# Spreading v over the key index by on-chip transfers into four slots in place of matmuls, with the normalised keys kept in PSUM, in a fused attention and mixture-of-experts layer

## The reference

```python
q = _silu(x @ Wq.T).reshape(b, n, H, HD)          # H = 16 heads, HD = 8
k = _silu(x @ Wk.T).reshape(b, n, H, HD)
v = _silu(x @ Wv.T).reshape(b, n, H, HD)
f = jax.nn.log_sigmoid(x @ Wf.T)
k = k / jnp.maximum(jnp.linalg.norm(k, axis=-1, keepdims=True), EPS_NORM)
# per head and token, in order of the tokens:
S = jnp.exp(ft)[..., None, None] * S + kt[..., :, None] * vt[..., None, :]
o = jnp.einsum('bhk,bhkv->bhv', qt, S)
...
# then: o normalised, gated with sigmoid(x @ Wg1.T @ Wg2.T), times Wo, added to x;
# layer norm and modulation; two shared experts and the best 2 of 8 experts per token,
# each silu(x @ w1.T) * (x @ w3.T) @ w2.T, hidden size 256; added to x
```

## Time and profile before

| | |
|---|---|
| three runs | 440.51 median, 438.13 to 441.07 us |
| profiled execution | 441.05 us, span 439.2 (1.85 us outside it) |
| PE busy | 382.0 us (87%), weight loads 292.8 (67%) beside it |
| DVE / ACT / POOL busy | 326.2 (74%) / 202.5 (46%) / 291.3 (66%) |
| starts of normalise_k, blocks 0 to 7 | 20.83, 45.05, 72.53, 105.43, 133.90, 161.86, 189.99, 217.97 us |

### The profile page before, as it was taken

One profiled execution on the slowest core, in us unless ns is written; L12 is line 12 of the kernel. 1 busy time (PEld: TensorE's weight loads), 2 busy tenths in 40 slices (PEclk: granted clock), 3 DMA queues, 4 the chain that ended last, 5 costly groups with the idle time before them and its releaser, 6 DMA issues. The chain is left out here.

```text
span 439.2 us, 8647 instructions
## 1 busy us (share of the span) xinstructions
PE 382.0 (87%) x2304; PEld 292.8 (67%) x2304; DVE 326.2 (74%) x941; ACT 202.5 (46%) x505; POOL 291.3 (66%) x373
## 2 busy tenths in 40 slices
PE   7768796869999999999987789788998998999875
PEld 3453453556775966868656468675887887888475
DVE  5789999876998989989899763534665665666535
ACT  3453343544456455553523343314554554555630
POOL 1155555785888887888968578752876878588600
PEclk8999999877999999999999598899999999999999
DMA  8800021000000000100000011122333333232197
GB/s 246 306 1 0 1 74 48 24 1 2 12 32 7 26 24 14 32 7 26 24 14 30 8 37 44 55 61 67 91 92 86 87 91 85 76 91 69 58 346 208
DMA packets 27808, 28.57 MB, mean 65 GB/s; under 512 B 4458, under 2 KB 21746, under 8 KB 27618
## 3 DMA queue, kind: packets, MB, share of 16 engines
q1 hardware_dynamic: 23442, 19.14, 15.0%
q0 software_dynamic: 4320, 8.89, 6.2%
HBM read 17.03 MB, written 12.03 MB: 66 GB/s over the span
## 5 line engine op out<-in xcount | busy, mean ns | idle before, releaser
L1406 POOL DMA_INDIRECT y_dram<-S x71 | 70.9, 999 | 17.7 <-issue 15.9
L1233 POOL TENSOR_TENSOR qS<-S,qT 128x512 f32<-128x512 f32 x56 | 74.3, 1330 | 10.4 <-DVE S L1550 10.2
L1255 POOL DMA_INDIRECT h_dram<-h,target_i x56 | 55.8, 996 | 15.4 <-issue 15.4
L1793 DVE COPY qS<-ff 128x256 f32<-128x256 f32 x71 | 30.2, 425 | 41.6 <-PE ff L880 41.6
L1537 DVE TENSOR_TENSOR at<-at,khat 128x512 f32<-128x512 f32 x64 | 44.0, 691 | 3.7 <-PE at L587 2.9
L1182 ACT ACTIVATE S<-ff 128x256 f32<-128x256 f32 x71 | 27.3, 384 | 34.4 <-PE ff L873 34.4
L1550 DVE TENSOR_TENSOR_SCAN S<-decay,S,at 128x512 f32<-128x512 f32 x32 | 40.8, 1274 | 0.6
L1550 DVE TENSOR_TENSOR_SCAN S<-decay,at 128x512 f32<-128x512 f32 x32 | 38.7, 1213 | 0.6
L1047 ACT ACTIVATE work<-ff 128x512 f32<-128x512 f32 x32 | 19.0, 595 | 39.3 <-PE ff L510 38.5
L871 PE MATMUL ff<-w_hi,vT_lo 128*128 x71 | 34.2, 482 | 3.2 <-issue 3.2
L586 PE MATMUL at<-vT_hi,spread_v 128*128 128x512 f32 x64 | 30.4, 476 | 7.2 <-DVE S L1550 5.6
(11 more groups left out here) (276 smaller groups left out, 1004.8 us busy)
## 6 DMA issues: line engine op xcount, KB each, us to landing
S<-h_dram SPq DMA_DIRECT2D x71, 64.5 KB, 1.9
xall<-in_x SPq DMA_DIRECT2D x8, 256.0 KB, 5.5
work<-in_w13T SPq DMA_DIRECT2D x8, 256.0 KB, 2.8
w_hi<-y_dram SPq DMA_DIRECT2D x8, 256.0 KB, 5.5
w_lo<-y_dram SPq DMA_DIRECT2D x8, 256.0 KB, 6.0
out<-xall SPq DMA_DIRECT2D x8, 256.0 KB, 3.1
w_sb<-in_w2T SPq DMA_DIRECT2D x1, 1280.0 KB, 6.8
y_dram<-S POOLq DMA_INDIRECT x71, 2.3
```

The costliest lines, as they stand in the source:

```text
L1233: pool.tensor_tensor(qS[:, v, :], S[:, v, :], qT[:, b % 2, :], ALU.mult).then_inc(s_qS, 1)
L1255: pool.indirect_dma_start(out=h_dram[:, :], out_offset=bass.IndirectOffsetOnAxis(ap=target_i[:, b % 2, k, t:t + 1], axis=0), in_=token_row ...
L1406: pool.indirect_dma_start(out=y_dram[:, :], out_offset=bass.IndirectOffsetOnAxis(ap=rows[:, u, P:P + 1].bitcast(I32), axis=0), in_=y_sb[:, ...
L1793: dve.tensor_copy(t_GT[:, u % RING, :], ff[2 + u % 2][:, 0:HID]).then_inc(s_tGT, 1)
```

## The change

v is no longer spread by PE. vT keeps two blocks (by b % 2), and SP's queue issues one transfer for each block and v: 16 rows of vT, those of value v, each copied to the 8 rows of its head in slot n % 4 of a new SBUF buffer `vs`, n = 8 b + v. A transfer waits until ACT has made vT of the block (s_act) and until update n-4 has read the slot. The six weight loads stand between the transfers of blocks 1 and 2. The parts of vT and `spread_v` are gone, with `split_v` on ACT and POOL.

`update` multiplies slot and keys into at[v%2], and waits for the transfer and for the scan that read the bank before. The keys stay in PSUM: `normalise_k` writes `kbank`, which is the bank that held the gathers' result (obank), and waits for updates 6 and 7 of the block before; update 7 of a block moves from the head of the next period to ahead of `normalise_k`. The gathers go to another bank (`bbank`), which the second silu pair and h also use, and both halves of block i-1 run in period i, between projections. v is projected second (ORDER), and ACT makes it ahead of the decay. The last query has a buffer of its own (q7). In the first period and period 1 matmuls without use (`keep_busy`) are placed anew; later periods have none.

```diff
-        ORDER = (1, 3, 2, 4, 0)
+        ORDER = (1, 2, 3, 4, 0)
...
+            def spread(b, v):
+                n = HD * b + v
+                if v == 0:
+                    sp.wait_ge(s_act, 5 * b + 2)
+                if n >= SPREAD:
+                    old_b, old_v = divmod(n - SPREAD, HD)
+                    sp.wait_ge(s_upd[half(old_v)], scans(old_b, old_v))
+                sp.dma_start(vs[:, n % SPREAD, :], vT[v:P:HD, b % 2, :].unsqueeze(1).broadcast_to([H, HD, TB])) \
+                    .then_inc(s_vs[n % SPREAD], 16)
...
+            for b in range(NB):
+                for v in range(HD):
+                    spread(b, v)
+                    if b == 1 and v >= HD // 2:
+                        load_w13(NSH + v - HD // 2 + 2)
+                    if b == 2 and v % 4 == 3:
+                        load_w13(NSH + v // 4 + 6)
...
             def gather(b, k):
                 if k == 0:
-                    wait(pe, s_og, b)
                     wait(pe, s_qS, (HD - 1) * b + HD // 2)
...
+                    if b < NB - 1:
+                        wait(pe, s_hrow, b - 1)
+                    else:
+                        pe.wait_ge(s_h2T, NB - 1)
...
             def period(i):
-                if i != 2:
-                    on(spread, i, 0)
                 on(up, i - 3, 2)
...
                 on(project, i + 1, 0)
-                on(spread, i, 1)
-                on(spread, i, 2)
+                on(gather, i - 1, 0)
                 on(project, i + 1, 1)
                 on(gather, i - 1, 1)
...
                 on(project, i + 1, 3)
                 on(logits, i - 2)
                 if i == 1:
-                    keep_busy(obank, 5)
-                on(spread, i, 6)
-                if i == 1:
-                    keep_busy(obank, 2)
-                on(spread, i, 7)
+                    keep_busy(ff[1], 7)
                 on(up, i - 2, 0)
...
                 on(transpose_x1, i + 2)
-                on(gather, i, 0)
...
             def update(b, v):
                 if v == 0:
                     wait(dve, s_khat, b + 1)
-                wait(dve, s_vb, HD * b + v + 1)
-                dve.tensor_tensor(at[half(v)][:, :], at[half(v)][:, :], khat[:, b % 2, :], ALU.mult).then_inc(s_upd[half(v)], 1)
+                n = HD * b + v
+                dve.wait_ge(s_vs[n % SPREAD], 16 * (n // SPREAD + 1))
+                wait(dve, s_scan[half(v)], scans(b, v) - 1)
+                dve.tensor_tensor(at[half(v)][:, :], vs[:, n % SPREAD, :], kbank[:, :], ALU.mult).then_inc(s_upd[half(v)], 1)
...
             def normalise_k(b):
                 wait(dve, s_rnT, b + 1)
-                wait(dve, s_red, 2 * (b - 1))
-                dve.scalar_tensor_tensor(khat[:, b % 2, :], abank[:, :], 1e12, kT[:, :], ALU.min, ALU.mult).then_inc(s_khat, 1)
+                if b == 0:
+                    dve.wait_ge(s_act, 4)
+                for v in (HD - 2, HD - 1):
+                    wait(dve, s_upd[half(v)], scans(b - 1, v))
+                dve.scalar_tensor_tensor(kbank[:, :], abank[:, :], 1e12, kT[:, :], ALU.min, ALU.mult).then_inc(s_khat, 1)
...
             def period(i):
-                on(update, i - 1, 7)
                 on(update, i, 0)
...
                 on(scan, i, 6)
+                on(update, i, 7)
                 on(normalise_k, i + 1)
```

More of the change, by code:

```diff
@@ L83 @@
 LOAD = 2
+SPREAD = 4
 DIAG_LATE, KEEP = 4, 7
@@ L250, in build @@
         t_GT = qS[:, 0:2, :].rearrange("p a (r n) -> p (a r) n", n=HID)
-        t_hi, t_lo = (a[:, :].rearrange("p (r n) -> p r n", n=P) for a in (vT_hi, vT_lo))
+        t_hi, t_lo = (vs[:, n, :].bitcast(F32R).rearrange("p (r n) -> p r n", n=P) for n in range(2))
         y_in = [a[:, 0:NB, :].bitcast(F32) for a in (w13_hi, w13_lo)]
@@ L305, in build @@
         s_khat = sem("s_khat")
-        s_vb = sem("s_vb")
+        s_vs = [sem(f"s_vs{n}") for n in range(SPREAD)]
         s_qS = sem("s_qS")
@@ L600, in gather @@
                     v = k * HD // 2 + n
-                    product = qS[:, v, :] if v < HD - 1 else khat[:, b % 2, :]
-                    ins = pe.matmul(obank[n * NQ:(n + 1) * NQ, :], gather_v[:, k, :], product, start=(k == 0), stop=(k == 1),
+                    product = qS[:, v, :] if v < HD - 1 else q7[:, :]
+                    ins = pe.matmul(bbank[n * NQ:(n + 1) * NQ, :], gather_v[:, k, :], product, start=(k == 0), stop=(k == 1),
                                     tile_position=(0, n * NQ))
@@ L757, in first_period @@
                 k_norms(1)
-                spread(0, 4)
                 project(1, 2)
-                spread(0, 5)
                 project(1, 3)
-                keep_busy(obank, 3)
-                spread(0, 6)
+                pe.wait_ge(s_act, 5)
+                keep_busy(bbank, 4)
                 project(1, 4)
-                spread(0, 7)
-                gather(0, 0)
+                keep_busy(bbank, 3)
                 transpose_rn(1)
@@ L820, in drain @@
                 up(a, 2)
+                gather(c, 0)
                 gather(c, 1)
@@ L966, in take_decay @@
                 wait(act, s_scan[1], scans(b - 2, HD - 1))
[L967 removed]
+                activate(b, 2, decay[:, b % 2, :], ACT.Tanh, 0.5)
             def finish_decay(b):
[L970 removed]
+                wait(act, s_act, 5 * b + 3)
                 act.activation(decay[:, b % 2, :], decay[:, b % 2, :], ACT.Copy, bias=0.5, scale=0.5).then_inc(s_decay, 1)
             def take_v(b):
[L974 to L980 removed]
+                for v in (HD - 2, HD - 1):
+                    wait(act, s_upd[half(v)], scans(b - 2, v))
+                activate(b, 1, vT[:, b % 2, :], ACT.Silu)
             def take_gate(b):
@@ L1688, in first_period @@
                 fold_gain_a()
+                update(0, 7)
                 normalise_k(1)
@@ L1740, in drain @@
                 link = Chain(dve, s_tab, 0)
-                update(c, 7)
                 scan(c, 7)
```

60 lines of the change are left out of this document (16 added, 44 removed).

## The result

The changed kernel took 454.32 us (median of four runs, 452.62 to 456.16) against 440.79 for the kernel before (438.13 to 442.08): ratio 1.0316, interval 1.0253 to 1.0379, so 3.2% slower. The direction is the forecast's; the time lies outside its range. The profiled execution took 454.67, with a span of 452.8, 13.6 more than before.

The account below looks back on a forecast made before the run. A once-per-period loop through four engines, without the spreads, was taken as the bound. From 441.05: keys +0.8, transfers 0, period 2 -0.7, drain +1.0 gave 442.1; two clock falls of 1.8 made 445.7 us, range 435 to 452.

Parts of the forecast that it names:

- The loop: Chain through four engines, closing once per period, sets the period's length; PE's spreads are not on it.
- Rival C (faster): DVE is the scarce engine and keeps saved waits for spread and silu: 434 to 437 us, chance 0.19.
- a term that stood at 0: Spreads leaving PE free 0.48 us a pair, 3.8 us a period, but gain 0 in time.
- The term for the keys: Update 7 ahead of the keys delays the next transposes: +0.2 us a period, +0.8 over four.
- The transfers at 0 in steady periods: Each 256 KB transfer on SP's queue takes 2.8 us, fits its slot's 14 us on average, and costs 0.
- The late weight load: In periods 1 and 2 a spread's transfer stands behind a load waiting for POOL: above 450 us, chance 0.09.
- The price of a fall: At the lower clock, up 0 takes +1.24 us and the projection behind it +0.6: 1.8 us a fall.
- the 28 to 29.5 us that were given as a sign: Expected spacing between starts of the key normalisation in the four steady periods of the changed kernel's profile.
- I assume that it falls in two of the four steady periods: TensorE's clock falls at up 0 after a new pause, in two steady periods: 2 x 1.8 us.
- -0.7 in period 2: Half of the 1.3 us that DVE's gating waited for a gather in period 2 is saved.
- +1.0 for the gathers in the drain: Both halves of the gathers now stand together ahead of the last block's gating: +1.0 us, between 0 and 1.2.
- Rival B's upper end: Clock falls in steady periods, 444 to 452 us, chance 0.39; four falls lasting through up 1 give 454.

Follow-up runs that it names:

- e12: The changed kernel with useless matmuls ahead of up 0 and the h2-row transposes, wide ones in period 2, and the last two weight loads earlier: 446.83 us.
- e5: The kernel before with update 7 of a block moved ahead of the next block's key normalisation, spreads still on PE, no transfers: 444.40 us.
- e4: The kernel before with the 64 transfers added, unread by anything, and the weight loads interleaved as in the changed kernel: 446.12 us.
- e3: The kernel before with the spreads of blocks 2 to 7 left out, no transfers, keys in SBUF: 454.50 us.
- e1: The changed kernel with four small useless matmuls between the logits and up 0 in periods 2 to 7: 447.57 us.
- e7: The changed kernel with four small useless matmuls ahead of up 0 and four more ahead of the transposes of h2's rows: 446.94 us.
- e9: The kernel before with the 64 unread transfers added and the last two weight loads issued two transfers earlier than in the changed kernel: 441.46 us.
- e2: The changed kernel with eight small useless matmuls between the logits and up 0 in periods 2 to 7: 446.65 us.
- e8: The kernel before with useless matmuls in period 2, two ahead of the projection of k and four ahead of the h2-row transposes: 442.28 us.

## Why the prediction was wrong, point by point

**The loop: right.** POOL, up 0, the silu, the product, the keys and hT follow each other after the change as the prediction had them, and the spreads lay off it: DVE's freed waits became waits for silu (2.0 us also without a fall, in e12's period from 131.55), and the busy share of PE was worth nothing. Rival C (faster) had no run on its side. One reading was off, in a term that stood at 0: the two pairs of spreads ahead of up 0 held PE from 184.27 to 185.46, so 0.6 us a pair and not 0.48.

**The term for the keys: right.** +0.2 a period; e5 measured 0.16 to 0.18 in three periods and none in the fourth. In the changed kernel without falls it was 0.0 to 0.6 for all edits but the clock together.

**The transfers at 0 in steady periods: right** (e4, 112.5). The late weight load was named as a rival's mechanism; it was real in e4 and not seen to cost in the changed kernel.

**The price of a fall: right for up 0 and the projection.** 1.24 and 0.58 measured in the period that ends at 166.55, 1.8 forecast. In three of the four periods it lasted through up 1 or began ahead of up 0, and the periods grew by 0.8, 2.0, 2.6 and 3.3 us; the 28 to 29.5 us that were given as a sign held in one of the four.

**The first step that failed: "I assume that it falls in two of the four steady periods".** It fell in all four. The pause was foreseen, 1.78 us for 1.8. With four falls the prediction's own sum is 442.1 + 4 x 1.8 = 449.3, still in its range, and its steady periods would have grown by 7.2 + 0.8 = 8.0; they grew by 8.7. That is 4.3 of the 8.9 us between the forecast and the profiled execution. I had taken the number of falls from one stretch of before that had a pause without a fall (64 to 72), and treated it as even odds, though the pause comes in the same place of every period. It also tied the fall to the pause ahead of up 0 alone; in two of the four periods the clock was down as the logits ended. The Trainium skill, page "TensorE: Matmul & The Clock Gate", section "HAM oscillation — how this bites in real kernels", tells of a kernel whose PE waits for transfers between bursts and starts each burst slow. The trace agrees as to every period, with 0.94, 0.87, 0.89 and 0.85 in the four, and differs as to the start: in two of them up 0 began at the full clock and slowed within 1 us.

**The second step that failed: the sum applied the clock to the steady periods alone.** Outside them it put +0.3 (-0.7 in period 2, +1.0 for the gathers in the drain). The changed kernel lost 4.9 us there, and that is what took the time past the range: 0.8 in period 2, at a clock of 0.65 for 0.79, and 3.0 behind the keys of block 7. By the starts of the expert loop (312.6 for 298.9) all of the 3.0 lies ahead of it, 84.1 us for 80.9 at a clock of 0.86 for 0.89, and the loop itself takes 106.1 for 106.5. What causes that part isn't settled: the same stretch lasts 220.2 to 222.6 us in the profiles of the kernels with the old drain, and 220.8 to 224.3 with the new one, at clocks from 0.95 to 0.98, so the gathers' share of it can't be told from where the clock happened to fall. Rival B's upper end, 454 for four falls that last through up 1, is the time measured; that agreement is luck, since the steady periods then would have grown by 13.0 and not by 8.7.

## What to carry to other kernels

Work of an engine that is off the critical path can still be worth its time: on TensorE it holds the clock up for the work behind it that is on the path, so before moving matmuls away, look at what PE does in the stretch ahead of each of its steps on the path, at all its pauses there and not only the last one, and don't count on a new pause that comes in every period passing without a fall in some of them. To test it cheaply, leave the work out (e3) and put useless work in its place (e1, e7). And a wait that a change removes is worth something only if the engine behind it has nothing later to wait for.

## What the runs showed of the hardware

64 transfers of 256 KB from SBUF to SBUF, each reading 16 partitions eight times over, landed after 3.0 us (median) beside all other work in the changed kernel; such transfers of constants, one after another, cost the kernel before nothing that could be measured (e9, ratio 0.9992, 0.9961 to 1.0022). Useless matmuls that are running when the clock falls run at the lower level themselves and, standing ahead in the list, delay what they were to speed up (e2: 1.5 us between the end of POOL's part and up 0). The clock fell without any pause just ahead: in e2 while the fill ran (0.50 from 160 to 162), and in the changed kernel as the logits ended (0.79 from 158 to 159). In the profile of e8 useless work in one period moved the fall into the next.
